# One-core vision block with sparse experts: GpSimd waits behind every second indirect DMA

## Chip, cores and metric

One Trainium2 chip, one core, one launch. The metric is the device time of the launch in microseconds (us), median of three runs. All arithmetic is in float32 apart from a few one-hot and triangular matrices.

## What is computed

64 images of 3x96x96 are cut into 16x16 patches, embedded to 192 features and given a class token, so there are 37 tokens an image and 2368 in all. An attention layer follows, then a sparse layer in which every token chooses 4 of 128 "feature" matrices and 4 of 128 "restore" matrices by its own router:

```python
w_fk, _ = topk_sparsify(softmax(logits_fk), 4)      # per token, over 128 experts
w_rk, _ = topk_sparsify(softmax(logits_rk), 4)
h   = einsum('bsnr,bsn->bsr', einsum('bsd,ndr->bsnr', x, f_know), w_fk)   # 192 -> 128
out = einsum('bsnd,bsn->bsd', einsum('bsr,nrd->bsnd', h, r_know), w_rk)   # 128 -> 192
return h_in + out
```

The kernel doesn't multiply every token with every matrix. It sorts copies of the token rows by expert in device memory, multiplies the sorted rows block by block, and brings the products back to token order.

## The kernel before, in words

**Attention.** Eight groups of eight images go through embedding, attention and residual (lines up to L1666). The tokens come out as 19 tiles of 128 rows. They form two batches, `BATCHES`: tiles 0 to 10 and tiles 11 to 18.

**Sorting.** When the router has chosen, VectorE (DVE) works out for each token and each choice the row ("slot") where its copy goes (`slot`, L1853, result at L1870). GpSimd (POOL) then writes the rows: `scatter_x2` (L691) issues four indirect DMAs a tile at L699, one for each choice, each moving 128 rows. For batch 0 that is 44 DMAs, for batch 1 it is 32. In the program the scatters come after all of GpSimd's work for the attention groups.

**Four expert phases.** `PHASES` is (layer 0, batch 0), (layer 0, batch 1), (layer 1, batch 0), (layer 1, batch 1), called phase 0 to 3 here. In each, SyncE (SP) loads blocks of sorted rows (L480), TensorE (PE) transposes them (L1124) and multiplies them (the fixed blocks at L1139, the data-dependent ones at L1150), ScalarE (ACT) copies out of PSUM (L1416, L1407) and SP stores the products (L496). SP's program is in one order: before phase 0 it waits until all of batch 0 is scattered (L560), before phase 1 for the scatters of batch 1 (`rows_of_second`), before phases 2 and 3 for the second scatter of batch 0 and of batch 1 (`mid_rows`). For phases 1 and 3 these waits stand ahead of the last loads and stores of the phase before. At the end of a phase SP waits for its stores and raises `experts_done` (L549). Between phases 1 and 2 the second layer's matrices are loaded over the first layer's (L485); PE waits for them at L1159.

**GpSimd beside the phases.** After phase 0 GpSimd fetches the products of batch 0: `gather` (L708) issues four indirect DMAs a tile at L712 into one of two buffers. DVE weights and sums the four (`combine`, L1902, lines L1911 and L1919) into `comb`. `scatter_mid` (L716) sends `comb` to the slots of the second layer with four indirect DMAs at L720. The order is gather, gather, then by turns a scatter and the gather of two tiles on. So 88 DMAs of batch 0 are issued beside phase 1 and the matrix load, and 64 of batch 1 beside phase 2. After phase 2 the second-layer products of batch 0 are gathered (44 DMAs, beside phase 3), and after phase 3 those of batch 1 (32 DMAs, the "last gathers"), summed by DVE and stored at L581.

GpSimd's waits in these functions are on work of others (`slot_ready`, `mid_ready`, `rows_ready`, `experts_done`); behind its own DMAs it waits for nothing. `take(pool)` (L364) is a semaphore increment that carries the wait standing ahead of it.

Of the kernel before, what the change touches and what calls it, by code (L numbers as in the profile page):

```python
# [46 lines left out]
BATCHES = ((0, READY[5]), (READY[5], TTILES))  # L47
# [47 lines left out]
def tower(nc, x, cls_tok, tok_w, tok_b, qkv_w, qkv_b, ln_g, ln_b,  # L95
          f_know, r_know, w_fk, b_fk, w_rk, b_rk, emb_fk, emb_rk, out):
    ctx = ExitStack()
    with ctx:
# [5 lines left out]
        def sem(name):  # L104
            return ctx.enter_context(nc.semaphore(name))
# [239 lines left out]
        scattered = [sem(f"scattered{t}") for t in range(BATCHES[0][1])] + [sem("scattered_rest")]  # L345
# [12 lines left out]
        gathered = [[sem(f"gathered{p}_{i}") for i in range(2)] for p in range(2)]  # L358
        mid_ready = sem("mid_ready")
        mid_out = [sem(f"mid_out{i}") for i in range(2)]  # L360
# [3 lines left out]
        def take(engine):  # L364

            engine.sem_inc(taken, 1)
# [219 lines left out]
        def _(pool):  # L586
# [104 lines left out]
            def scatter_x2(b, t):  # L691
                if t == BATCHES[b][0]:
                    pool.wait_ge(zeroed[b], 16 * len(ZEROED[b]))
                pool.wait_ge(slot_ready, t + 1)
                if b == 1:
                    pool.wait_ge(xb_ready, t - BATCHES[1][0] + 1)
                take(pool)
                for e in range(TOPK):
                    pool.indirect_dma_start(wide_dram[b], bass.IndirectOffsetOnAxis(ap=slots[:, t, e:e + 1], axis=0),  # L699
                                            x2b[:, t - BATCHES[b][0], :], None)\  # L700
                        .then_inc(scattered[min(t, BATCHES[0][1])], 16)

            for g in range(GROUPS - 1):
                group(g, min(3, GROUPS - 1 - g))
                for t in SCATTERED[g]:
                    scatter_x2(0, t)

            def gather(layer, b, t):  # L708
                i = t % 2
                for e in range(TOPK):  # L710
                    k = layer * TOPK + e
                    pool.indirect_dma_start(gat[i][:, e, :], None, wide_dram[b],  # L712
                                            bass.IndirectOffsetOnAxis(ap=slots[:, t, k:k + 1], axis=0))\
                        .then_inc(gathered[layer][i], 16)

            def scatter_mid(b, t):  # L716
                pool.wait_ge(mid_ready, t + 1)
                take(pool)
                for e in range(TOPK):
                    pool.indirect_dma_start(mid_dram[b],  # L720
                                            bass.IndirectOffsetOnAxis(ap=slots[:, t, TOPK + e:TOPK + e + 1], axis=0),
                                            comb[t % 2][:], None).then_inc(mid_out[t % 2], 16)

            for b, (lo, hi) in enumerate(BATCHES):
                for t in range(lo, hi):
                    if t not in sum(SCATTERED.values(), []):
                        scatter_x2(b, t)
            for i in (2, 3):
                pool.wait_ge(zeroed[i], 16 * len(ZEROED[i]))
            for b, (lo, hi) in enumerate(BATCHES):  # L730
                pool.wait_ge(experts_done[b], 1)
                pool.wait_ge(mid_slot_ready, TTILES)
                take(pool)
                for t in range(lo, min(lo + 2, hi)):
                    gather(0, b, t)
                for t in range(lo, hi):
                    scatter_mid(b, t)
                    if t + 2 < hi:
                        gather(0, b, t + 2)
            for b, (lo, hi) in enumerate(BATCHES):  # L740
                pool.wait_ge(experts_done[2 + b], 1)
                take(pool)
                for t in range(lo, hi):
                    if t >= 2:
                        pool.wait_ge(rows_ready, t - 1)
                        take(pool)
                    gather(1, b, t)
# [3 lines left out]
        def _(pe):  # L751
# [357 lines left out]
            def experts(ph):  # L1109
# [55 lines left out]
                with pe.Fori(FIXED, ALL_STEPS) as s, pe.If(s < used):  # L1165
                    _, starts = nc.values_load_multi_w_load_instructions(
                        owner[0:1, b, layer, bass.ds((s - FIXED) * BODY, BODY)], engines=[mybir.EngineType.PE],
                        min_val=0, max_val=(EXPERTS - 1) * (256, D)[layer],
                        skip_runtime_bounds_check_because="owner is clamped to the experts where it is computed")
                    for r in range(RING):  # L1170
                        if r + 1 < RING:
                            transposed(s, r + 1)
                        else:
                            with pe.If(s + 1 < used):
                                transposed(s + 1, 0)
                        products(s, r, starts)
# [258 lines left out]
        def _(dve):  # L1435
# [171 lines left out]
            def keep_factors(columns):  # L1607
                _, c1, ts = columns
                if ts:
                    lo, hi = ts[0], ts[-1] + 1  # L1610
                    dve.tensor_copy(rs2[:, lo:hi], rr[:, TILES:c1])
                    dve.scalar_tensor_tensor(nb2[:, lo:hi], mv2[:, lo:hi, 0], -1.0, rr[:, TILES:c1], ALU.mult, ALU.mult)\
                       .then_inc(nb2_ready, 1)
# [337 lines left out]
```

## Time and profile before

| | us |
|---|---|
| median of 3 timed runs | 784.07 (784.05 to 784.77) |
| span of the profiled execution, first to last instruction | 1062.3 |
| GpSimd: gathers L712 (x152), busy | 146.3 |
| GpSimd: scatters L699 (x76), busy | 75.2 |
| GpSimd: scatters L720 (x76), busy | 74.9 |
| PE busy, share of the span | 583.6, 55% |

The profiled execution's span is longer than a timed run of the same kernel; beyond its span nothing of its own time is shown. How to read the rows further down: a row of the timeline is start, duration, engine, line, operation, what it writes and reads, and in brackets how long the engine sat idle before it and what ended that. "issue" is a wait for nothing that the profile shows. The duration of a DMA_INDIRECT row is GpSimd's own; the data land later. A matmul in float32 counts as two in the profile.

### The profile page before, as it was taken

To read this page: it belongs to the slowest core of one execution; us is meant where nothing else is said; L and a number is where in the kernel's file an instruction comes from. 1 tells how busy PE (TensorE), PEld (TensorE's weight loads), DVE (VectorE), ACT (ScalarE), POOL (GpSimd) and SP (SyncE) were. 2 spreads that over 40 slices of the span, in tenths; PEclk is the share of its full clock that TensorE was granted. 3 is DMA by queue.
4 is the path that set the end of the run, shared out by engine and by line. 5 is a ranking of instruction groups with operands and counts; after the bars stand their busy time and mean duration, and the time that the engine had idled before them with its cause. 6 is when DMAs were issued, how large, how long until landed. Compare 5 with 4: busy or idle time off the path is not lost.

```text
span 1062.3 us, 16453 instructions
## 1 busy us (share of the span) xinstructions
PE 583.6 (55%) x5060; PEld 453.4 (43%) x5061; DVE 387.7 (36%) x1412; ACT 339.6 (32%) x738; POOL 403.1 (38%) x397
## 2 busy tenths in 40 slices
PE   7888998999863534298631115960410576217600
PEld 6677786787642313178510003760300265003500
DVE  3666887887884845290011110000111000330013
ACT  3445575657521330055300002530100353004400
POOL 4413443143135536500077770000677101770065
PEclk9699999998965656599855556985755698558955
DMA  5987768860941963267532223689722475335652
GB/s 139 358 349 261 277 256 346 321 276 18 174 96 63 192 155 108 77 178 196 141 95 64 66 74 83 180 237 282 208 76 63 125 221 157 100 91 171 183 148 76
DMA packets 163730, 177.44 MB, mean 167 GB/s; under 512 B 12777, under 2 KB 147218, under 8 KB 163666
## 3 DMA queue, kind: packets, MB, share of 16 engines
q1 hardware_dynamic: 150290, 149.20, 45.8%
q0 software_dynamic: 13376, 27.41, 8.8%
q8 instruction: 36, 0.59, 0.2%
q14 instruction: 28, 0.23, 0.1%
HBM read 76.55 MB, written 100.02 MB: 166 GB/s over the span
## 4 chain that ended last, share of the span: by engine, by line
PE 32%; issue 25%; another core or an unknown queue 12%; ACT 10%; DVE 9%; SPq 5%; DMA 4%; POOL 2%; ACTq 0%; POOLq 0%; DVEq 0%
PE bank L1139 8%; PE bank L855 5%; PE bank L1150 4%; PE bank L1124 4%; ACT qk_pad L1240 3%; PE bank L902 3%; POOL gat L712 2%; SPq L496 2%; PE bank L840 1%; DVE smax L1634 1%; PE bank L1157 1%; SPq L485 1%; PE bank L963 1%; ACT xsT L1416 1%
## 5 line engine op out<-in xcount | busy, mean ns | idle before, releaser
L712 POOL DMA_INDIRECT gat<-wide_dram,slots x152 | 146.3, 962 | 365.1 <-SPq L549 320.0
L1139 PE MATMUL bank<-matrices,xsT 96*32 96x128 f32 (+1 forms) x1536 | 98.9, 330 | 226.1 <-issue 174.9
L1407 ACT ACTIVATE os<-bank 128x256 f32<-128x256 f32 (+1 forms) x160 | 69.9, 438 | 384.5 <-remote 230.1
L1139 PEld LDWEIGHTS bank<-matrices,xsT 96*32 96x32 f32 (+1 forms) x1536 | 51.7, 120 | 263.7 <-issue 201.3
L1124 PE MATMUL bank<-ident,xs 128*96 128x128 f32 (+1 forms) x480 | 91.6, 300 | 59.4 <-issue 39.5
L1911 DVE TENSOR_SCALAR acc<-gat,wts 128x128 f32<-128x128 f32 x19 | 5.4, 286 | 311.6 <-DMA gat<-wide_dram,slots 191.7
L1416 ACT ACTIVATE xsT<-bank 96x512 f32<-96x512 f32 (+1 forms) x160 | 76.4, 487 | 91.9 <-PE bank L1124 53.7
L699 POOL DMA_INDIRECT wide_dram<-x2b,slots x76 | 75.2, 989 | 71.1 <-issue 38.8
L1150 PE MATMUL bank<-matrices,xsT 96*128 (+1 forms) x576 | 97.3, 308 | 2.6 <-ACT xsT L1416 2.3
L1124 PEld LDWEIGHTS bank<-ident,xs 128*96 128x96 f32 (+1 forms) x480 | 56.2, 139 | 90.3 <-issue 72.3
L656 POOL TENSOR_TENSOR qk_sum<-qk_pad 64x888 f32<-64x888 f32 x16 | 26.6, 1665 | 167.6 <-ACT qk_pad L1240 156.6
L720 POOL DMA_INDIRECT mid_dram<-comb,slots x76 | 74.9, 985 | 25.5 <-issue 22.8
L1150 PEld LDWEIGHTS bank<-matrices,xsT 96*128 96x128 f32 (+1 forms) x576 | 80.0, 198 | 9.7 <-issue 7.4
L1919 DVE SCALAR_TENSOR_TENSOR acc<-gat,wts,h2r 128x192 f32<-128x192 f32 x19 | 8.0, 419 | 204.4 <-DMA gat<-wide_dram,slots 198.4
L855 PE MATMUL bank<-tok_wT,pixT 128*128 128x192 f32 x384 | 69.5, 342 | 1.3 <-ACT pixT L1217 1.3
L855 PEld LDWEIGHTS bank<-tok_wT,pixT 128*128 128x128 f32 x384 | 67.5, 202 | 2.4 <-ACT pixT L1217 1.6
L1865 DVE SCALAR_TENSOR_TENSOR pick<-iota_n,idxf,srank 128x128 f32<-128x128 f32 x152 | 44.6, 349 | 4.2 <-DVE srank L1862 3.0
L902 PE MATMUL bank<-w_vT,xnT_rep 96*111 96x192 f32 x256 | 44.7, 335 | 2.3 <-ACT xnT_rep L1228 2.3
L1259 ACT ACTIVATE probs<-probs 101x444 f32<-101x444 f32 x32 | 18.3, 572 | 82.3 <-DVE probs L1637 82.1
L902 PEld LDWEIGHTS bank<-w_vT,xnT_rep 96*111 96x111 f32 x256 | 43.2, 181 | 2.8 <-ACT xnT_rep L1228 2.7
L1157 PE MATMUL bank<-ones,ident 128*128 128x128 f32 x104 | 18.6, 362 | 42.1 <-DMA matrices<-in_L_ffn_r_know 31.1
L1240 ACT ACTIVATE qk_pad<-bank,qk_bias,qk_scale 64x296 f32<-64x296 f32 x64 | 38.0, 593 | 6.8 <-PE bank L885 5.8
(187 smaller groups left out, 973.5 us busy)
## 6 DMA issues: line engine op xcount, KB each, us to landing
wide_dram<-zeros SPq DMA_DIRECT2D x6, 5632.0 KB, 19.5
mid_dram<-zeros SPq DMA_DIRECT2D x8, 2816.0 KB, 25.9
xs<-wide_dram SPq DMA_DIRECT2D x80, 192.0 KB
wide_dram<-os SPq DMA_DIRECT2D x80, 192.0 KB, 2.3
matrices<-in_L_ffn_f_know SPq DMA_DIRECT2D x8, 1536.0 KB
matrices<-in_L_ffn_r_know SPq DMA_DIRECT2D x8, 1536.0 KB, 11.8
wide_dram<-os SPq DMA_DIRECT2D x80, 128.0 KB, 2.6
xs<-mid_dram SPq DMA_DIRECT2D x80, 128.0 KB
```

The source lines that it names most:

```text
L699: pool.indirect_dma_start(wide_dram[b], bass.IndirectOffsetOnAxis(ap=slots[:, t, e:e + 1], axis=0), x2b[:, t - BATCHES[b][0], :], None)\
L712: pool.indirect_dma_start(gat[i][:, e, :], None, wide_dram[b], bass.IndirectOffsetOnAxis(ap=slots[:, t, k:k + 1], axis=0))\
L720: pool.indirect_dma_start(mid_dram[b], bass.IndirectOffsetOnAxis(ap=slots[:, t, TOPK + e:TOPK + e + 1], axis=0), comb[t % 2][:], None).the ...
L855: last = pe.matmul(bank[2 + 3 * f][:, t * D:(t + 1) * D], pixT[:, half, c, 2 * j:2 * j + 2, :].rearrange("p a n -> p (a n)"), tok_wT[:, kt ...
L902: last = pe.matmul(bank[VALUE_BANK[f]][0:VG * TOK, t * D:(t + 1) * D], xnT_rep[:, j * G_IMG + m].rearrange("p r n -> p (r n)"), w_vT[:, j, ...
L1124: last = pe.transpose(bank[r % 2][0:kp, c:c + ROWS], src, ident[:])
L1139: last = pe.matmul(bank[2 + r][q * FIRST:(q + 1) * FIRST, k * width:(k + 1) * width], xsT[r % 2][0:kp, c:c + FIRST], matrices[0:kp, at:at ...
L1150: last = pe.matmul(bank[2 + r][:, k * width:(k + 1) * width], xsT[r % 2][0:kp, c:c + ROWS], matrices[0:kp, bass.ds(starts[r * SB + k] + j ...
L1240: ins = act.activation(qk_pad[g % 2][half, m * G_IMG:(m + 1) * G_IMG, 1:1 + TOK], src, ACT.Identity, bias=qk_bias[half, m:m + 1], scale=qk ...
L1407: act.activation(os_[r][:, :, 0:width], bank[2 + r][:, 0:SB * width].rearrange("p (k w) -> p k w", w=width), ACT.Copy)\
L1416: act.activation(dst, src, ACT.Copy).then_inc(t_copied[ph], 1)
L1865: last = dve.scalar_tensor_tensor(pick[:, k, :], iota_n[:], idxf[:, t, r, k:k + 1], srank[:, 0:EXPERTS], ALU.is_equal, ALU.mult, accum_out ...
```

## The change

Behind every second indirect DMA of a tile GpSimd waits on the semaphore of these DMAs until both have landed. This holds for both scatters and for the gathers of layer 0 and of layer 1, batch 0; the last gathers (layer 1, batch 1) stay as they are. Each tile's four DMAs get two such waits.

```diff
@@ scatter_x2
                         .then_inc(scattered[min(t, BATCHES[0][1])], 16)
+                    if e % 2 == 1:
+                        pool.wait_ge(scattered[min(t, BATCHES[0][1])], 64 * max(t - BATCHES[0][1], 0) + 16 * (e + 1))
+                        take(pool)
@@ gather
                         .then_inc(gathered[layer][i], 16)
+                    if e % 2 == 1 and (layer == 0 or b == 0):
+                        pool.wait_ge(gathered[layer][i], 64 * (t // 2) + 16 * (e + 1))
+                        take(pool)
@@ scatter_mid
                                             comb[t % 2][:], None).then_inc(mid_out[t % 2], 16)
+                    if e % 2 == 1:
+                        pool.wait_ge(mid_out[t % 2], 64 * (t // 2) + 16 * (e + 1))
+                        take(pool)
```

## Rows read from the trace of the kernel before

**Rows 1.** Cores: span from the first to the last instruction and mean granted clock.

```profile
core 0: 1062.3 us, clock 0.749
```

**Rows 2.** Busy time by stretch: from:to, length, busy us (instructions) by engine, clock, DMA, GB/s.

```profile
409.00:446.00 37.00, 8.01 (x24) 2.76 (x24) 9.22 (x55) 0.00 (x0) 25.75 (x27) 0.55 0.24 80
...
538.00:648.00 110.00, 18.90 (x52) 6.53 (x52) 13.54 (x40) 1.96 (x4) 78.19 (x81) 0.50 0.22 66
648.00:709.00 61.00, 49.81 (x647) 41.29 (x647) 0.00 (x0) 27.03 (x57) 0.00 (x0) 0.86 0.62 172
...
760.00:834.00 74.00, 6.54 (x54) 2.69 (x54) 8.04 (x24) 2.52 (x6) 50.99 (x53) 0.53 0.25 74
...
909.00:962.00 53.00, 6.87 (x36) 2.40 (x36) 16.76 (x40) 2.68 (x8) 34.91 (x36) 0.50 0.30 82
962.00:1014.00 52.00, 36.64 (x332) 24.41 (x332) 0.00 (x0) 25.21 (x63) 0.00 (x0) 0.93 0.66 200
```

The engines stand in the order PE, PE weight loads, DVE, ACT, POOL.

**Rows 3.** Timeline of PE, phase 0, during and after the scatters of batch 1.

```profile
431.16 0.37 PE L1139 MATMUL bank<-matrices,xsT 96*32 96x128 f32 x1 [1.72 <-issue]
...
449.30 1.94 PE L1139 MATMUL bank<-matrices,xsT 96*32 96x128 f32 x32
```

**Rows 4.** Chain that ended last, from 314 to 400 us: start, length, what.

```profile
326.52 15.70 another core or an unknown queue
...
374.82 5.83 another core or an unknown queue
...
382.50 3.13 another core or an unknown queue
```

**Rows 5.** Timeline of POOL: first and last indirect DMA of each stage, and two between.

```profile
313.84 1.19 POOL L699 DMA_INDIRECT wide_dram<-x2b,slots  x1 [17.47 <-issue]
...
382.40 0.96 POOL L699 DMA_INDIRECT wide_dram<-x2b,slots  x1 [0.30 <-issue]
...
528.42 0.98 POOL L712 DMA_INDIRECT gat<-wide_dram,slots  x1 [85.74 <-SPq L549]
...
532.23 0.95 POOL L712 DMA_INDIRECT gat<-wide_dram,slots  x1 [0.30 <-issue]
...
639.60 0.96 POOL L720 DMA_INDIRECT mid_dram<-comb,slots  x1 [0.30 <-issue]
743.17 0.98 POOL L712 DMA_INDIRECT gat<-wide_dram,slots  x1 [102.61 <-SPq L549]
...
746.98 0.95 POOL L712 DMA_INDIRECT gat<-wide_dram,slots  x1 [0.30 <-issue]
...
825.86 0.97 POOL L720 DMA_INDIRECT mid_dram<-comb,slots  x1 [0.31 <-issue]
898.96 0.98 POOL L712 DMA_INDIRECT gat<-wide_dram,slots  x1 [72.13 <-SPq L549]
...
953.66 0.95 POOL L712 DMA_INDIRECT gat<-wide_dram,slots  x1 [0.30 <-issue]
1014.11 0.95 POOL L712 DMA_INDIRECT gat<-wide_dram,slots  x1 [59.50 <-SPq L549]
```

**Rows 6.** Timeline of SP: the first loads of phase 0 and the first of phase 3.

```profile
399.52 8.69 SPq L480 DMA_DIRECT2D xs<-wide_dram  x6
...
890.41 0.37 SPq L480 DMA_DIRECT2D xs<-mid_dram  x1
```

**Rows 7.** Timeline of DVE: the first sum of tile 0 and of tile 11.

```profile
534.94 0.29 DVE L1911 TENSOR_SCALAR acc<-gat,wts 128x128 f32<-128x128 f32 x1 [54.50 <-DMA gat<-wide_dram,slots]
...
753.32 0.29 DVE L1911 TENSOR_SCALAR acc<-gat,wts 128x128 f32<-128x128 f32 x1 [119.92 <-issue]
```

**Rows 8.** Timeline of DVE and POOL: GpSimd's restart after a wait.

```profile
401.19 0.16 DVE L1870 SCALAR_TENSOR_TENSOR slots<-idxf,slotf 128x4 int32<-128x4 f32 x1
...
402.16 0.96 POOL L699 DMA_INDIRECT wide_dram<-x2b,slots  x1 [18.80 <-DVE slots L1870]
```

## The prediction, made before the changed kernel was run

> **What bounds the kernel now.** I read the spans first. The profiled execution spans 1062.3 us [rows 1] and the median of the timed runs is 784.07, so 278 us of the span are not in a timed run. That has to be explained before any row may carry a price.
>
> The second view is the busy time by stretch [rows 2]. While GpSimd issues indirect DMAs, the others hardly run: from 538 to 648 us PE does 52 matmuls, in the 61 us after that 647. The same is seen from 409 to 446, 760 to 834 and 909 to 962. The timeline shows how: during the scatters one matmul of 0.37 us starts 1.72 us after the last, "issue", with no wait ahead of it; when they are over, 32 go in 1.94 us [rows 3]. The DMA engines are not full there (share 0.22 to 0.30), so they don't explain it. Earlier, the chain of waits has three stalls of the same kind, 15.70 + 5.83 + 3.13 = 24.7 us [rows 4].
>
> I now rebuild the time without these stalls. Work that PE did in a stalled stretch is charged at the rate of a free one: 61/647 = 0.094 us a matmul in layer 0, 52/332 = 0.157 in layer 1 [rows 2]. GpSimd's pace is (639.60 + 0.96 - 528.42)/88 = 1.27 us a DMA [rows 5].
> - To the first load of phase 0: 399.5 [rows 6] - 24.7 = 374.8.
> - Phase 0, up to GpSimd's first gather: 128.9 - 37 + 24 x 0.094 = 94.2.
> - Phase 1 and the matrix load, 528.42 to 743.17: 214.8 - 110 + 52 x 0.094 = 109.7. GpSimd's 88 DMAs beside it take 112.1, so 112.1.
> - Phase 2, 743.17 to 898.96: 155.8 - 74 + 54 x 0.157 = 90.3. GpSimd: 83.7 (743.17 to 826.83), 1.8 until landed (below), and 8.6 from the first load of phase 3 at 890.41 [rows 6] to the next gather, 94.1 in all. So 94.1.
> - Phase 3, 898.96 to 1014.11: 115.2 - 53 + 36 x 0.157 = 67.9. GpSimd: 55.7.
> - Last gathers to the end: 48.2.
>
> The sum is 791.3; with GpSimd's two terms left out, 785.1. Both are within 1% of 784.07. So the timed runs are accounted for with **no stall at all**: I read the stalls as something that the profiled execution has and the timed runs don't. What bounds the timed kernel from phase 1 on is then two things that finish almost together: the expert phases (109.7 and 90.3) and GpSimd's train of DMAs (112.1 and 94.1).
>
> One rule bears on what the stalls are. The Trainium skill (NOTIFIC — the notification-queue block, section on overflow) says that the block which takes the trace records holds its producers back inside rather than lose a record. By that the stalls go with the recording and their cure is worth nothing in a timed run; by the rows alone they could be real and worth up to 278 us, were the sum above not closed without them. No row shows the record path itself.
>
> **The change, part by part.** It adds two waits for each tile's four DMAs: 22 for the scatters of batch 0, 16 for those of batch 1, 44 and 32 beside phases 1 and 2, and 22 for the gathers beside phase 3. It removes and moves nothing. What is queued behind each wait is GpSimd's next DMA; DVE's sums, SP's `mid_rows` and so the next phase wait for that.
>
> Price of a wait. No row of before shows GpSimd waiting for its own DMA, so I bound it. The fourth gather of tile 0 ends on GpSimd at 533.18 [rows 5] and DVE starts on it at 534.94 [rows 7]: landed 1.76 us later. GpSimd's restart after a semaphore takes 0.81 (401.35 to 402.16) [rows 8]. Without a wait the gap is 0.30 [rows 5]. So a wait adds at least 1.76 - 0.30 = 1.46, if the restart costs nothing more, and at most 1.76 + 0.81 - 0.30 = 2.27. I take the middle, **1.85**, as part of the 1.76 is DVE's own start. Next to the matrix load landing took 5.39 (747.93 to 753.32) [rows 5, 7]: 3.6 more a pair; a pair then takes 2 x 1.27 + 1.85 + 3.6 = 8.0, and the load of some 34 us holds four, so 15 us more, which goes into the upper end only.
>
> The stages with 1.85 a pair:
> - Scatters of batch 0 start at 313.84 and need 44 x 1.27 + 22 x 1.85 = 96.6: done at 410.4 where SP could load at 374.8. In the profile they have slack (they end at 383.36 [rows 5], before 399.5); without stalls that is gone. **+36**.
> - Scatters of batch 1, 32 x 1.27 + 16 x 1.85 = 70, lie beside phase 0's 94: 0. If phase 0 had under 70, the rest would show.
> - Batch 0 beside phase 1: 112.1 + 44 x 1.85 = 193.5 for 112.1: **+81**. The matrix load is hidden long before.
> - Batch 1 beside phase 2: 83.7 + 32 x 1.85 + 8.6 = 151.5 for 94.1: **+57**. Phase 2's own 90 is covered.
> - Gathers beside phase 3: 55.7 + 22 x 1.85 = 96.4 for 67.9: **+28**. The last gathers queue behind them on GpSimd.
> - The last gathers: nothing is added.
>
> Together 410.4 + 94.2 + 193.5 + 151.5 + 96.4 + 48.2 = 994.2, 203 over 791.3. From the median: **987 us**. By the same sums 1.46 gives 156 more (940), 2.27 gives 253 (1037), and with the matrix load 1052. The lower end: if timed runs let GpSimd go 15% quicker (pace 1.08, wait 1.24), the stages are 388.6, 94.2, 149.9, 119.4, 74.6, 48.2, in all 875 against 785, +90: 874.
>
> A second rule speaks for the change. The Trainium skill (DMA: Bandwidth & Descriptors, "Queues, rings and completion order") says that each DMA engine takes turns between its queues, so a backlog of indirect DMAs would hold up SP's loads, and bounding it would help. The trace disagrees: from 538 to 648 the DMA share is 0.22 [rows 2], so there is no backlog to bound. By the rule some microseconds would come back; by the row none, and I count none.
>
> **The rivals.**
> 1. The waits hide. If GpSimd's pace in timed runs is half of the profile's (0.64) with a wait of 1.46, its stages are 374.1 (374.8 without), 56 + 64 = 120 (110), 41 + 47 + 9 = 97 (90) and 28 + 32 = 60 (68): some 17 us more, 801; with the wait halved too, no change, 784. For it: 785.1 closes without GpSimd's terms. Against it: its DMAs take 0.95 to 0.98 in stalled stretches and in the last gathers alike, so the stalls don't slow it. Chance 0.09, of which 0.04 for no change.
> 2. Faster: the stalls are partly real. The place is beside phases 1 to 3; a wait leaves the other engines free for 1.85 of each 4.4 us, and gives back 42% of what is stalled. It decides only where this is more than GpSimd's train lengthens, so GpSimd must be quick as in rival 1 (17 us) and real stalls must exceed 40 us. With a quarter of 278, 70 us, the change gives back 29 and costs 17: 772. For it: the stalls are plain in every stage. Against: the rebuilt sum has no room for 70 us. Chance 0.06.
> 3. The change doesn't do what it says, because a count is met before the landing. I exclude it from the code: a tile's four DMAs are the only ones that count on that semaphore at the time, and the thresholds count them.
>
> **How the numbers follow.** The forecast, GpSimd's train as the bound, has 0.83, and 0.02 more lie above its upper end, where landing is slower everywhere. The range 870 to 1055 is that case with the bounds of the wait, of GpSimd's pace and of the matrix load; rivals 1 and 2 and the 0.02 stay outside. Slower by over 0.2% (about what a measurement of this kernel can tell from no change): 0.83 + 0.05 + 0.02 = 0.90. Within 0.2%: 0.04. Faster: 0.06.
>
> **What the changed profile would show.** GpSimd's DMAs in pairs: 0.30 us idle before one, 1.8 to 2.6 before the next, ended by the pair's landing. 88 DMAs beside phase 1 in 175 to 215 us instead of 112; PE idle ahead of phases 2 and 3, waiting for SP, which waits for the second scatter. The last gathers unchanged. The stalls of PE should thin out in the profile, so that its span may hardly grow, or shrink, while the time grows: span and time come closer. I'd be wrong if the gaps are under 1 us, if PE's phases still end later than GpSimd's train, or if the time falls as the span does.

## The result and the profile after

The changed kernel takes **1102.57 us** (median of 4 runs, 1094.69 to 1103.91), the kernel before, timed beside it, 784.42: a ratio of 1.4027 (95% interval, in brackets from here on: [1.3964, 1.409]), slower by 318 us. The forecast was 987 with a range up to 1055. The profiled execution of the changed kernel took 1103.05 us and spans 1101.3. The kernel before was profiled again (first experiment) and then spans 779.6, so the 1062.3 of [rows 1] was an untypical execution; all comparisons by stage below use the second profile.

The busy time by stretch of the changed kernel (columns as in [rows 2]):

```profile
534.00:600.00 66.00, 50.73 (x752) 41.71 (x752) 4.07 (x12) 29.87 (x63) 21.25 (x22) 0.89 0.73 203
600.00:645.00 45.00, 13.42 (x79) 12.70 (x80) 2.68 (x8) 4.16 (x9) 11.63 (x12) 0.58 0.98 293
645.00:769.00 124.00, 3.43 (x27) 3.24 (x26) 8.05 (x24) 0.00 (x0) 52.30 (x54) 0.53 0.12 35
...
845.00:929.00 84.00, 0.00 (x0) 0.00 (x0) 5.37 (x16) 0.00 (x0) 35.88 (x38) 0.50 0.12 36
```

Phase 1 is nearly done by 600 us, the matrix load by 645. From there to 769 PE does 27 matmuls and from 845 to 929 none at all: everybody waits for GpSimd, whose 54 DMAs of the first of these stretches use 0.12 of the DMA engines. Unlike the stalls of [rows 2], this idling stands in the timed runs too.

The first lines of section 4 of the page of the changed kernel (the chain that ended last) and its groups of indirect DMAs:

```profile
DMA 35%; issue 18%; PE 14%; POOL 13%; DVE 11%; ACT 7%; SPq 1%; POOLq 0%; DVEq 0%; ACTq 0%
DMA gat<-wide_dram,slots 18%; DMA mid_dram<-comb,slots 9%; POOL gat L715 8%; DMA wide_dram<-x2b,slots 7%; PE bank L864 5%; POOL mid_dram L726 3%; ACT qk_pad L1249 3%; PE bank L911 3%; POOL wide_dram L699 2%; PE bank L849 1%; DVE smax L1643 1%; PE bank L979 1%; DVE pick L1874 1%; DVE probs L1646 1%; PE bank L972 1%
...
L715 POOL DMA_INDIRECT gat<-wide_dram,slots x152 | 145.5, 957 | 227.5 <-DMA gat<-wide_dram,slots 133.5
...
L699 POOL DMA_INDIRECT wide_dram<-x2b,slots x76 | 75.8, 997 | 144.4 <-DMA wide_dram<-x2b,slots 100.9
L726 POOL DMA_INDIRECT mid_dram<-comb,slots x76 | 74.3, 978 | 122.7 <-DMA gat<-wide_dram,slots 58.2
```

The landings of the three kinds of indirect DMA make 18 + 9 + 7 = 34% of the chain, some 375 us. The issue itself has not changed (957 to 997 ns). The idle time ahead of it is now ended by a landing.

GpSimd's timeline in the changed kernel; the number in brackets is the idle time ahead of the instruction, and who ended it. [Rows 5] answer to these lines:

```profile
319.04 1.19 POOL L699 DMA_INDIRECT wide_dram<-x2b,slots  x1 [15.78 <-issue]
...
328.35 0.96 POOL L699 DMA_INDIRECT wide_dram<-x2b,slots  x1 [2.26 <-DMA wide_dram<-x2b,slots]
...
534.18 0.98 POOL L715 DMA_INDIRECT gat<-wide_dram,slots  x1 [10.73 <-SPq L549]
...
609.62 1.01 POOL L726 DMA_INDIRECT mid_dram<-comb,slots  x1 [7.14 <-DMA gat<-wide_dram,slots]
610.93 0.98 POOL L726 DMA_INDIRECT mid_dram<-comb,slots  x1 [0.30 <-issue]
...
655.71 0.95 POOL L715 DMA_INDIRECT gat<-wide_dram,slots  x1 [2.44 <-DMA gat<-wide_dram,slots]
...
664.93 0.96 POOL L726 DMA_INDIRECT mid_dram<-comb,slots  x1 [2.08 <-DMA mid_dram<-comb,slots]
...
769.28 0.98 POOL L715 DMA_INDIRECT gat<-wide_dram,slots  x1 [2.23 <-DMA mid_dram<-comb,slots]
...
937.81 0.98 POOL L715 DMA_INDIRECT gat<-wide_dram,slots  x1 [9.99 <-SPq L549]
...
1052.99 0.95 POOL L715 DMA_INDIRECT gat<-wide_dram,slots  x1 [2.63 <-DMA gat<-wide_dram,slots]
1054.24 0.94 POOL L715 DMA_INDIRECT gat<-wide_dram,slots  x1 [0.31 <-issue]
```

The pattern is the forecast one: pairs, 0.30 inside a pair, a landing between pairs. But the gap has two sizes. Where the other engines are done (from 646 to 769) it is 2.07 to 2.23 behind scatters and 2.41 to 2.66 behind gathers. While SP loads and stores (534 to 645) it is 2.8 to 7.1, but for one of 2.06.

By stage, with the idle time that the waits add (each gap less the 0.30 that stands without a wait). The stages start at the lines above (534.18, 769.28, 937.81, 1052.99) and at SP's first load of phase 0, which is the first line here for the changed kernel and the second for the kernel before; the other three are starts of the second profile of the kernel before, and 465.26 stands in experiment 1:

```profile
437.84 4.97 SPq L480 DMA_DIRECT2D xs<-wide_dram  x6
```

```profile
377.86 7.28 SPq L480 DMA_DIRECT2D xs<-wide_dram  x6
...
579.03 0.98 POOL L712 DMA_INDIRECT gat<-wide_dram,slots  x1 [0.30 <-issue]
...
669.94 0.97 POOL L712 DMA_INDIRECT gat<-wide_dram,slots  x1 [9.93 <-SPq L549]
...
731.37 0.94 POOL L712 DMA_INDIRECT gat<-wide_dram,slots  x1 [2.88 <-SPq L549]
```

| stage | forecast | changed | before, 2nd profile | growth | waits, idle added |
|---|---|---|---|---|---|
| to the first load of phase 0 | 410.4 | 437.8 | 377.9 | 60.0 | 22, 61 |
| phase 0 to the first gather | 94.2 | 96.4 | 87.4 | 9.0 | 16, beside phase 0 |
| batch 0 beside phase 1 | 193.5 | 235.1 | 113.8 | 121.3 | 44, 123 |
| batch 1 beside phase 2 | 151.5 | 168.5 | 90.9 | 77.6 | 32, 78 |
| gathers beside phase 3 | 96.4 | 115.2 | 61.4 | 53.8 | 22, 60 |
| last gathers to the end | 48.2 | 48.3 | 48.2 | 0.1 | 0 |
| sum | 994.2 | 1101.3 | 779.6 | 321.7 | 120 charged, 322 |

(The second row's 16 waits are not among the 120.) 322/120 = 2.69 us a wait, where the forecast took 1.85.

### The profile page after: what moved, and what is told of

Read it like the earlier page. It is cut to its first block, busy times and chain, and to the rows that moved or that the text cites. A ratio compares the mean times of both kernels' runs of the same rounds, so it can differ in the third digit from the quotient of the medians.

```text
span 1101.3 us, 16589 instructions
## 1 busy us (share of the span) xinstructions
PE 547.0 (50%) x5060; PEld 443.1 (40%) x5061; DVE 385.9 (35%) x1412; ACT 340.6 (31%) x738; POOL 402.4 (37%) x397
## 4 chain that ended last, share of the span: by engine, by line
DMA 35%; issue 18%; PE 14%; POOL 13%; DVE 11%; ACT 7%; SPq 1%; POOLq 0%; DVEq 0%; ACTq 0%
DMA gat<-wide_dram,slots 18%; DMA mid_dram<-comb,slots 9%; POOL gat L715 8%; DMA wide_dram<-x2b,slots 7%; PE bank L864 5%; POOL mid_dram L726 3%; ACT qk_pad L1249 3%; PE bank L911 3%; POOL wide_dram L699 2%; PE bank L849 1%; DVE smax L1643 1%; PE bank L979 1%; DVE pick L1874 1%; DVE probs L1646 1%; PE bank L972 1%
## 5 line engine op out<-in xcount | busy, mean ns | idle before, releaser
L1133 PE MATMUL bank<-ident,xs 128*96 128x128 f32 (+1 forms) x480 | 88.7, 297 | 223.4 <-issue 129.3
L1133 PEld LDWEIGHTS bank<-ident,xs 128*96 128x96 f32 (+1 forms) x480 | 54.2, 138 | 251.6 <-issue 158.8
L864 PE MATMUL bank<-tok_wT,pixT 128*128 128x192 f32 x384 | 73.7, 356 | 1.3 <-ACT pixT L1226 1.3
L864 PEld LDWEIGHTS bank<-tok_wT,pixT 128*128 128x128 f32 x384 | 71.8, 213 | 2.5 <-ACT pixT L1226 1.6
L1166 PEld LDWEIGHTS bank<-ones,ident 128*128 128x128 f32 x104 | 20.0, 300 | 130.2 <-issue 130.2
L1148 PE MATMUL bank<-matrices,xsT 96*32 96x128 f32 (+1 forms) x1536 | 65.9, 308 | 11.8 <-ACT xsT L1425 11.8
L1148 PEld LDWEIGHTS bank<-matrices,xsT 96*32 96x32 f32 (+1 forms) x1536 | 41.4, 114 | 27.7 <-ACT xsT L1425 16.1
```

Source lines behind the costliest of these rows:

```text
L864: last = pe.matmul(bank[2 + 3 * f][:, t * D:(t + 1) * D], pixT[:, half, c, 2 * j:2 * j + 2, :].rearrange("p a n -> p (a n)"), tok_wT[:, kt ...
L1133: last = pe.transpose(bank[r % 2][0:kp, c:c + ROWS], src, ident[:])
L1148: last = pe.matmul(bank[2 + r][q * FIRST:(q + 1) * FIRST, k * width:(k + 1) * width], xsT[r % 2][0:kp, c:c + FIRST], matrices[0:kp, at:at ...
L1166: pe.matmul(bank[7][:, 0:ROWS], ident[:], ones[:], start=True, stop=True)
```

## The experiments

**1. The kernel before, profiled again.** No edit. What was expected:

> The kernel before, unchanged. Theory 'train' (GpSimd's row of DMAs with its waits sets the end; the stalls of the first profile are no part of a timed run): 784 us again, and the spans of the timed executions within 3 us of their times, about 782. A profile with a span of about 1062 and the stalls beside that would say that the stalls go with that profile alone; a profile of about 782 without them would say that the first one was not typical. Rival 'stalls': timed executions hold them too, their spans are near 1062 and the 784 is another quantity.

Measured: 783.62 us, ratio 1.0027 [0.9995, 1.0058]. The profiled execution took 781.29 and spans 779.6 us; the ten timed executions span 776.9 to 787.8, so the rival, that timed runs hold the stalls too, falls. Busy time by stretch, beside phases 1 and 3:

```profile
465.00:579.00 114.00, 69.84 (x844) 60.35 (x845) 15.13 (x44) 34.24 (x72) 84.91 (x88) 0.74 0.91 271
...
670.00:731.00 61.00, 41.40 (x404) 27.74 (x404) 16.91 (x41) 28.68 (x72) 41.86 (x44) 0.92 0.88 257
```

The timeline of GpSimd and DVE at the gathers of the first two tiles of the same kernel:

```profile
465.26 0.98 POOL L712 DMA_INDIRECT gat<-wide_dram,slots  x1 [44.30 <-SPq L549]
...
469.06 0.95 POOL L712 DMA_INDIRECT gat<-wide_dram,slots  x1 [0.30 <-issue]
...
471.88 0.28 DVE L1911 TENSOR_SCALAR acc<-gat,wts 128x128 f32<-128x128 f32 x1 [42.30 <-DMA gat<-wide_dram,slots]
...
474.06 0.95 POOL L712 DMA_INDIRECT gat<-wide_dram,slots  x1 [0.30 <-issue]
...
478.40 0.48 DVE L1911 TENSOR_SCALAR acc<-gat,wts 128x128 f32<-128x128 f32 x1 [5.08 <-DMA gat<-wide_dram,slots]
```

The stalls are gone: beside phase 1 PE does its matmuls while GpSimd issues 88 DMAs, at 1.29 us each where [rows 5] have 1.27. The rebuilt stages of the prediction (374.8, 94.2, 112.1, 94.1, 67.9, 48.2) and the measured ones differ by 7 us or less each. But two things the first profile had hidden show here. The DMA engines are at 0.91 beside phase 1, where [rows 2] have 0.22. And landing isn't one number: 471.88 - 470.01 = 1.87 us for the first tile, 478.40 - 475.01 = 3.39 for the second, and by the same reckoning 2.18 to 5.55 for the nine others beside phase 1. In the first profile all eleven tiles there come out at 1.66 to 1.76.

**2 to 4. One part of the waits each.** Against the changed kernel, only the waits in `scatter_x2` (2), only those of layer 0 in `gather` and `scatter_mid` (3), only those of the gathers of layer 1, batch 0 (4). The last as an example, with the arguments of the removed wait left out (`...`):

```diff
@@ scatter_x2, scatter_mid
-                    if e % 2 == 1:
-                        pool.wait_ge(...)
-                        take(pool)
@@ gather
-                    if e % 2 == 1 and (layer == 0 or b == 0):
+                    if e % 2 == 1 and layer == 1 and b == 0:
```

> Waits behind every second DMA of the first scatters alone. Theory 'train': the first loads of phase 0 wait for batch 0's scatters, at 438 us as in the changed kernel in place of 375; beside phase 0 the 32 scatters of batch 1 stay hidden. +63, about 847. Rival 'stalls': the waits free the other engines beside phase 0 as well, and the time stays within 20 of 784.

> Waits in the gathers of layer 0 and the second scatters alone (beside phases 1 and 2). Theory 'train': the stages take 235 and 169 us as in the changed kernel in place of 112 and 94: +197, about 981. Rival 'stalls': less than half of that, under 880, since phases 1 and 2 run undisturbed and give time back.

> Waits in the gathers of layer 1, batch 0 alone (beside phase 3). Theory 'train': 115 us in place of 68 for phase 3: +47, about 831. Rival 'hidden': GpSimd's 44 gathers have slack beside phase 3, +10 or less, under 795. The three parts together: 63 + 197 + 47 = 307 of the 318 measured, if they add up.

Measured: 844.86 (1.0808 [1.0768, 1.0848]), 981.5 (1.2554 [1.2509, 1.2599]) and 837.31 (1.0697 [1.0652, 1.0742]), against 782.2 for the kernel before, timed beside them. That is +62.7, +199.3 and +55.1, together 317 of the 318. The first two came out as expected, the third 8 us dearer than its +47. The parts add up: each stage loses its own waits, and having all of them neither wins nor costs anything more.

**5. Half as many waits**, one behind all four DMAs of a tile:

```diff
-                    if e % 2 == 1:
+                    if e == TOPK - 1:
```

> As the changed kernel, with one wait behind each tile's four DMAs in place of two. Theory 'train': half as many waits at the price each has in the changed kernel's trace (2.8 us in the stages of layer 0, batch 0, 2.4 in batch 1, 2.7 in layer 1). Scatters of batch 0 +28, phases 1 and 2 +60 and +37, phase 3 +24: about 149 more than 784, 933. Rival 'depth': what costs is not the number of waits but that four DMAs must land at once, the price doubles and the time stays near 1100. Rival 'restart only': under 860.

Measured: 951.43 (948.95 to 957.69), 1.2161 [1.2076, 1.2246]: +167 us for half the waits, 53% of the loss, and above what was expected. GpSimd's timeline beside phase 1 of this kernel:

```profile
608.58 1.02 POOL L726 DMA_INDIRECT mid_dram<-comb,slots  x1 [5.65 <-DMA gat<-wide_dram,slots]
...
615.51 0.97 POOL L715 DMA_INDIRECT gat<-wide_dram,slots  x1 [2.11 <-DMA mid_dram<-comb,slots]
...
622.85 1.02 POOL L726 DMA_INDIRECT mid_dram<-comb,slots  x1 [2.60 <-DMA gat<-wide_dram,slots]
```

Once the traffic is over (from 615) a wait costs the same behind four DMAs as behind two: 2.11 and 2.60, where the changed kernel has 2.08 and 2.44 to 2.66. So it is the number of waits that is paid for, not the number of DMAs waited for. Over the whole kernel a wait comes to 167/60 = 2.78, a little dearer than the 2.65 (318/120) of the changed kernel. The trace shows why: 24 of these 60 gaps are above 2.75 us (4.48 over the 0.30 in the mean), where the changed kernel has 40 of 120 (4.04), so more of the shorter train lies beside SP's traffic.

**6. A wait in a quiet place**: the waits only behind the last gathers, where no expert phase runs and where the change has none.

```diff
-                    if e % 2 == 1 and (layer == 0 or b == 0):
+                    if e % 2 == 1 and layer == 1 and b == 1:
```

(and none in the scatters).

> Waits behind every second DMA of the last gathers alone, which the change leaves out. No other engine moves data there but SP's stores of the result. Theory 'traffic' (a wait costs 1.85 to 2.3 where nothing else moves, and more only beside other transfers): 16 waits x 2.2 = +35, less what DVE's sums hide, 810 to 822. Rival 'fixed price': 16 x 2.75, the mean of the changed kernel's 120 waits = +44, 828.

Measured: 817.22 (816.65 to 823.1), 1.043 [1.037, 1.049], against 784.44. GpSimd's timeline there:

```profile
748.26 0.94 POOL L712 DMA_INDIRECT gat<-wide_dram,slots  x1 [2.60 <-DMA gat<-wide_dram,slots]
749.51 0.95 POOL L712 DMA_INDIRECT gat<-wide_dram,slots  x1 [0.30 <-issue]
752.91 0.94 POOL L712 DMA_INDIRECT gat<-wide_dram,slots  x1 [2.46 <-DMA gat<-wide_dram,slots]
```

Fifteen gaps, mean 2.57: 2.27 more than without the wait, 15 x 2.27 = 34 us, and 32.8 in the time, where 'fixed price' had 44. So the quiet price of a wait behind gathers is 2.27, the forecast's upper bound, and all of it shows.

**7. The wait one pair behind**: one wait among four DMAs, for those issued before them, so that landing and issue overlap (none for the scatters of batch 1). Two theories: what costs is the landing (then this is nearly free), or what costs is any wait, by GpSimd's restart.

```diff
@@ scatter_x2 (gather and scatter_mid in the same way)
-                    if e % 2 == 1:
-                        pool.wait_ge(scattered[min(t, BATCHES[0][1])], 64 * max(t - BATCHES[0][1], 0) + 16 * (e + 1))
+                    if e == 1 and b == 0 and t > 0:
+                        pool.wait_ge(scattered[t - 1], 64)
```

> One wait a tile, behind its second DMA, on the pair issued before this pair (56 waits in the stages of the change but the scatters of batch 1). Theory 'train': the older pair has landed by then, as landing ends 1.4 to 1.8 us behind the issue and a pair takes 2.5 to issue, so the wait costs next to nothing except beside the matrix loads: 784 to 805. Rival 'restart': every wait costs GpSimd its restart, 56 x 0.8 = +45, near 829, whatever it waits for.

Measured: 834.31 (828.96 to 839.4), 1.0622 [1.0553, 1.0692], near the number of the restart theory, but the trace shows another cause. GpSimd's timeline beside phase 1, beside the matrix load that follows and after both:

```profile
506.66 0.94 POOL L715 DMA_INDIRECT gat<-wide_dram,slots  x1 [2.00 <-DMA mid_dram<-comb,slots]
...
551.76 0.96 POOL L731 DMA_INDIRECT mid_dram<-comb,slots  x1 [4.53 <-DMA gat<-wide_dram,slots]
...
567.78 0.96 POOL L731 DMA_INDIRECT mid_dram<-comb,slots  x1 [3.33 <-DMA gat<-wide_dram,slots]
...
604.21 1.00 POOL L731 DMA_INDIRECT mid_dram<-comb,slots  x1 [0.30 <-issue]
605.51 0.98 POOL L731 DMA_INDIRECT mid_dram<-comb,slots  x1 [0.30 <-issue]
606.79 1.07 POOL L731 DMA_INDIRECT mid_dram<-comb,slots  x1 [0.30 <-issue]
608.17 0.96 POOL L731 DMA_INDIRECT mid_dram<-comb,slots  x1 [0.30 <-issue]
```

After the traffic, a wait that is already met leaves the gap at 0.30 (the four scatters from 604 hold one): a met wait is free, so the restart theory falls. Beside the matrix load (540 to 600 here, DMA engines at 0.98) the same wait stops GpSimd for 2.9 to 4.5 us in all but one tile's turn, although a pair's issue lies in between: there the landing is longer than the 2.5 us that two issues take. Beside the loads and stores of phase 1 itself (0.75) most of these waits still leave 1.0 to 2.2. That was the miss of the landing theory: it excepted the matrix loads without a price for them and took every other landing as a quiet one. By the gaps, some 36 us of idle time lie beside the two matrix loads and some 28 elsewhere, of which the time shows 50; that it came near the restart theory's 829 is chance.

**8. Less traffic beside the waits.** In the changed kernel SP's last three loads of the second set of matrices go behind `mid_rows(0)`, from beside phase 1 to the time after its last scatter:

```diff
-            for n in range(EXPERTS // CHUNK - EARLY):
-                load_r(EARLY + n, r_late[n])
             expert_end(1)
             mid_rows(0)
+            for n in range(EXPERTS // CHUNK - EARLY):
+                load_r(EARLY + n, r_late[n])
```

> The changed kernel with the last three of the eight loads of the second layer's matrices issued after the second scatter of batch 0 has landed, not before. Theory 'traffic' (a wait is dear where SP moves data at the same time): the four waits of 5 to 6.5 us that lie beside these three loads fall to 2.1 to 2.6, so the stage beside phase 1 takes 218 to 224 us in place of 235; the loads then lie beside the first gathers of batch 1, whose waits grow by about as much, so the whole time stays near 1102, between 1092 and 1112. Rival 'own landing' (the long waits come from GpSimd's own DMAs and not from the loads): the stage beside phase 1 stays at 235 and the whole grows by what phase 2 waits for its matrices, if anything.

Measured: 1098.75 (1094.28 to 1102.91), 1.4051 [1.3949, 1.4153]. GpSimd's timeline: the start of the stage, the stretch in which the changed kernel had gaps of 5.0 to 6.5, and the start of the next stage:

```profile
533.52 0.98 POOL L715 DMA_INDIRECT gat<-wide_dram,slots  x1 [10.12 <-SPq L549]
...
620.85 0.98 POOL L715 DMA_INDIRECT gat<-wide_dram,slots  x1 [6.29 <-DMA mid_dram<-comb,slots]
...
630.86 1.02 POOL L726 DMA_INDIRECT mid_dram<-comb,slots  x1 [2.57 <-DMA gat<-wide_dram,slots]
...
635.23 0.96 POOL L726 DMA_INDIRECT mid_dram<-comb,slots  x1 [2.06 <-DMA mid_dram<-comb,slots]
...
757.85 0.97 POOL L715 DMA_INDIRECT gat<-wide_dram,slots  x1 [2.24 <-DMA mid_dram<-comb,slots]
```

With the loads gone the gaps from 630 on are the quiet ones. The stage beside phase 1 is 757.85 - 533.52 = 224.3 instead of 235.1, where 218 to 224 had been expected of the traffic. The time doesn't show it: the loads now lie beside batch 1's DMAs, whose stage grows from 168.5 to 173.5, and the few microseconds left over are within the spread of the runs (1094 to 1104 for both kernels). So the gap follows the traffic, wherever it is put.

The chain of waits of the changed kernel splits the gap. One pair of scatters beside the matrix load, one as it ends (start, length, what):

```profile
610.93 6.38 DMA mid_dram<-comb,slots
...
617.36 0.76 issue
618.11 0.96 POOL mid_dram L726
...
643.62 2.25 DMA mid_dram<-comb,slots
...
645.90 0.76 issue
646.66 0.96 POOL mid_dram L726
```

The restart (the "issue" ahead of the next DMA) is 0.76 in both. The landing, counted from the start of the pair's second DMA, is 6.38 against 2.25.

## Why the prediction was wrong in size

**What held.** The direction and the mechanism: GpSimd's train of DMAs becomes the bound in every stage with waits but phase 0's, the last gathers are unchanged, the stalls of the first profile cost nothing in a timed run, and span and time come together (1101.3 and 1103.05). That the span "may hardly grow" came true only by the untypical first profile: from 1062.3 it grew by 39, from the second profile's 779.6 by 322. The stages add up (experiments 2 to 4). The rivals fall: the waits don't hide, and there are no stalls for them to cure. That the counts are met at the landing and not before shows in each gap.

**What failed: the price of a wait.** The prediction took 1.85 from the bounds 1.46 and 2.27 and charged it 120 times: 222 us. Measured are 322, or 2.69 a wait. The upper end of its range, 1055, fails with it: that has 2.27 a wait and a long landing for four pairs only, where 40 waits had one. The miss of 100 of the 107 us has two parts, by the gaps of the changed kernel:
- Quiet waits: 79 gaps of up to 2.7 us, 158.8 us over the 0.30, and the wait behind the last scatter of batch 1, which lies in a longer wait for SP and is taken as 1.8: 2.01 each, so 0.16 x 80 = 13 us. To take the middle "as part of the 1.76 is DVE's own start" was wrong: GpSimd pays its own restart of 0.76 to 0.81 in full behind the landing, as the chain shows. The upper bound was the right value for gathers (2.27 in experiment 6); scatters land sooner (2.08 - 0.30 = 1.78).
- Waits beside other transfers: 40 gaps above 2.7 us, 161.7 us, 4.04 each, so 2.2 x 40 = 88 us. The prediction had this in one place only, the matrix load, as 15 us, and left it out of the forecast. In fact it stands in four: 4 gaps among the scatters of batch 0, around SP's load of the first set of matrices (7.28, 7.90, 3.26 and 9.30; of the last the trace names DVE's slots as what ended it, but this tile's had been done 25 us before, and the longest landing there, 9.4 us, fills the gap), 15 beside phase 1, 11 beside phase 2 and 10 beside phase 3.

The root lies in the row that the price came from. [Rows 7] take the first tile's landing out of a profile in which, while GpSimd issued, the other engines stood almost still, with the DMA engines at 0.22 to 0.30 [rows 2]. I had concluded that those stalls aren't in the timed runs, and put PE's work back into the stages, but not SP's transfers beside GpSimd's, and so charged a landing time of idle queues. No other tile beside phase 1 would have told in that profile (1.66 to 1.76), and the first tile alone would have misled in the second one too (1.87 there, 2.18 to 5.55 for the others). The 5.39 us of tile 11 was the one row of a landing under load. Its line ends the wait with "issue" and names no landing, though DVE waits there for nothing but that tile's gathers. It should have warned that every landing beside a phase's loads and stores is longer; as a price for all of them, 5.39 + 0.81 - 0.30 = 5.90, it would have been too dear: 4.04 is what such a wait measured in the mean.

With 80 waits at 2.01 and 40 at 4.04 the prediction's own sum would have been 994.2 + 100 = 1094, against 1101.3 measured; 5.2 of the rest is the first scatter's later start (319.04 against 313.84; in the other traces it lies between 313.23 and 320.76).

**The smaller terms.** The scatters of batch 1 were charged nothing. In the changed kernel SP's timeline has a pause in phase 0:

```profile
508.53 0.39 SPq L496 DMA_DIRECT2D wide_dram<-os  x1
524.91 0.37 SPq L480 DMA_DIRECT2D xs<-wide_dram  x1
```

SP stands for 16 us and goes on just after the last of these scatters has landed (it ends on GpSimd at 523.45): `rows_of_second` waits for it. Phase 0 grows by 9.0. The prediction's condition ("if phase 0 had under 70") was set for a train of 70 us; at these gaps it is 84.8 (438.69 to 523.45).

**The rules.** The Trainium skill (DMA: Bandwidth & Descriptors, "Queues, rings and completion order") says that each DMA engine takes turns between its queues. The prediction drew from it that a backlog of indirect DMAs would hold up SP's loads, and answered that there is "no backlog to bound", from the share of 0.22. That reading was of the untypical execution: in the second profile the share beside phase 1 is 0.91, and the first scatters land after 6.0 us (median) without waits and 2.5 with them:

```profile
wide_dram<-x2b,slots POOLq DMA_INDIRECT x76, 6.0
```

```profile
wide_dram<-x2b,slots POOLq DMA_INDIRECT x76, 2.5
```

No run here shows the turns themselves. The waits do shorten the landing of the scatters, but no stage came out shorter, and the conclusion of no gain held.

The other rule, of the Trainium skill (NOTIFIC — the notification-queue block, section on overflow), is that the block which takes the trace records holds its producers back inside rather than lose a record. The second profile was recorded too and has no stalls, so recording alone doesn't bring them. No row shows the record path, and what brought them in that one execution wasn't found.

## What to carry to other kernels

A wait for one's own DMA costs the landing plus the restart, each time, on the engine that issues: in this kernel 2.1 to 2.7 us of idle engine in a quiet stretch and 2.8 to 9.3 beside other transfers, against 0.30 with no wait or with one that is already met. Price a wait from a landing row of a stretch that is as loaded as the one the wait will stand in. Where a profile's span doesn't fit the timed runs, not only its idle times are suspect, but also every latency read from it, since the load is missing too.

## What the runs showed of the hardware

- How long a pair of indirect DMAs takes to land depends on what else moves: from the start of the second, 2.2 to 2.7 us with the DMA engines at 0.12 of their time (645 to 769 in the changed kernel), and 5.09 to 7.13 with them at 0.98 (600 to 643).
- A wait costs the same behind four quiet DMAs as behind two (2.60 against 2.44 to 2.66).
- GpSimd's restart behind a landing is 0.76 to 0.81 us, in quiet and loaded stretches alike, and behind a met wait the gap is the 0.30 that stands without one.
- Of the two profiled executions of the kernel before, the first was 283 us longer (1062.3 against 779.6), with the stalls of [rows 3]; the second has none.
